# First cross attention of a two-layer perceiver: its first two batches prepared in the latents' program, the last context rows' chain earlier, the bias tile by tile

## The reference, cut to what matters

```python
xn = layernorm(x, ln_x_g, ln_x_b)          # context, 257 rows a batch
ln = layernorm(latents, ln_l_g, ln_l_b)    # latents, 32 rows a batch
q = ln @ Wq
kv = concat([xn @ Wkv, ln @ Wkv], axis=1)  # keys and values of both
qn = rmsnorm(q, qn_g) * scale
kn = rmsnorm(k, kn_g)
attn = softmax(qn kn^T)                    # mask is all ones
out = attn @ v
return out @ Wout + bout
```

## Time and profile before

| | |
|---|---|
| median of 3 runs | 2802.11 us (2801.28 to 2806.9) |
| profiled execution | 2826.43 us, span 2824.7 us |
| mean granted TensorE clock | 0.943 |
| PE busy | 2516.9 us, 89% |
| DVE, ACT, POOL busy | 60%, 45%, 52% |
| latents' program | 0 to 219.8 us |
| first cross attention's preparation | 219.8 to 277.7 us |

### The profile page before, as it was taken

How to read it: one execution, slowest core, us unless ns; L and a number is a source line. 1 busy time by engine, 2 the same in 40 slices (tenths; PEclk the granted TensorE clock), 3 DMA queues, 4 the chain that set the end, 5 groups by cost and what they waited for, 6 DMA issues and landing times. The chain is left out here.

```text
span 2824.7 us, 67316 instructions
## 1 busy us (share of the span) xinstructions
PE 2516.9 (89%) x24481; PEld 1963.2 (70%) x24481; DVE 1708.8 (60%) x3971; ACT 1280.7 (45%) x2967; POOL 1459.7 (52%) x1623
## 2 busy tenths in 40 slices
PE   5884999999999999999687989489999999998986
PEld 2443878787878787877465568378888888885654
DVE  5663767575757675866366653456556656554662
ACT  3551646464646464656243323144454444543431
POOL 4774757575757474767364135455456543322220
PEclk9996999999999999999798899799999999999995
DMA  4332111121111111111000629542234323210000
GB/s 147 126 116 66 44 34 44 30 46 28 46 28 46 29 46 33 42 37 28 26 4 4 216 78 294 173 134 88 81 96 99 80 69 72 75 33 15 3 4 30
DMA packets 221891, 190.06 MB, mean 67 GB/s; under 512 B 88513, under 2 KB 208979, under 8 KB 221587
## 3 DMA queue, kind: packets, MB, share of 16 engines
q1 hardware_dynamic: 205442, 150.88, 18.0%
q0 software_dynamic: 10656, 31.05, 4.6%
q10 hardware_dynamic: 5488, 3.94, 0.5%
HBM read 151.49 MB, written 34.31 MB: 66 GB/s over the span
## 5 line engine op out<-in xcount | busy, mean ns | idle before, releaser
L840 POOL TENSOR_TENSOR rk<-ss,neg_half 128x32 f32<-128x32 f32 x64 | 347.6, 5432 | 211.8 <-DVE ss L746 211.8
L940 ACT ACTIVATE score<-score,ntop 128x289 f32<-128x289 f32 x256 | 135.4, 530 | 255.4 <-DVE ntop L757 252.6
L1024 PE MATMUL banks<-x_hi,wk_hi 128*128 128x256 f32 x1024 | 219.5, 297 | 32.1 <-DVE kT L740 31.4
L1544 PE MATMUL banks<-rowsT,qk 128*128 128x257 f32 x1024 | 243.1, 380 | 0.8 <-ACT qk L1471 0.8
L1024 PE MATMUL banks<-x_hi,wk_lo 128*128 128x256 f32 x1024 | 211.4, 289 | 0.0
L1024 PE MATMUL banks<-x_lo,wk_hi 128*128 128x256 f32 x1024 | 210.6, 288 | 0.0
L1544 PEld LDWEIGHTS banks<-rowsT,qk 128*128 128x128 f32 x1024 | 189.4, 190 | 27.8 <-ACT qk L1471 1.5
L740 DVE COPY kT<-banks 128x512 f32<-128x512 f32 x256 | 176.1, 688 | 52.5 <-PE banks L1024 50.9
L918 ACT ACTIVATE ksq<-kT 128x512 f32<-128x512 f32 x256 | 161.2, 630 | 85.6 <-DVE kT L740 83.7
L1024 PEld LDWEIGHTS banks<-x_hi,wk_hi 128*128 128x128 f32 x1024 | 163.9, 197 | 35.6 <-DVE kT L740 25.5
L1365 POOL DMA_INDIRECT parts<-scratch_expert,address x128 | 131.7, 1029 | 93.5 <-DVE residual L1263 45.9
(11 more groups left out here) (375 smaller groups left out, 6645.7 us busy)
## 6 DMA issues: line engine op xcount, KB each, us to landing
rowsT<-in_ctxT SPq DMA_DIRECT2D x64, 257.0 KB
raw<-in_ctx SPq DMA_DIRECT2D x64, 256.0 KB
wgu<-in_expert_gu SPq DMA_DIRECT2D x64, 256.0 KB
rows<-in_ctx SPq DMA_DIRECT2D x64, 256.0 KB
scratch_qT<-qT SPq DMA_DIRECT2D x16, 512.0 KB, 2.6
scratch_kT<-kT SPq DMA_DIRECT2D x16, 512.0 KB, 3.2
q<-scratch_qT SPq DMA_DIRECT2D x64, 128.0 KB
kT<-scratch_kT SPq DMA_DIRECT2D x64, 128.0 KB
```

The source lines that it names most:

```text
L840: nc.gpsimd.tensor_tensor(m.rk[:], m.ss[:], kit.neg_half[:, 0:KF * H], ALU.pow).then_inc(s.rk, 1)
L940: nc.scalar.activation(m.score[:, c, :], m.score[:, c, :], ACT.Exp, bias=m.ntop[:, c:c + 1], accum_out=m.mass[:, c:c + 1]).then_inc(s.p, 1)
L1024: mm = nc.tensor.matmul(key_bank[i % 2][:, a * ROWS:(a + 1) * ROWS], w[:, f, pr * P:(pr + 1) * P], x[:, k, f, :], start=(at == 0), stop=(a ...
L1544: mm = nc.tensor.matmul(score[h][:, c - h * HALF, 0:CTX], m.qk[:, f, j, c * BT:(c + 1) * BT, :].rearrange("p h q -> p (h q)"), m.rowsT[:, ...
```

## The change

It moves the cross program's preparation into the latents' program, moves the last rows' chain from steps 14 and 15 to steps 0 to 3, and cuts the bias add in tiles.

- The buffers, semaphores and PSUM banks of the preparation go into a class `KeyedFront` made outside both programs, and its pieces into functions (`keyed_vector`, `keyed_pool`, `keyed_scalar`, `keyed_tensor`) that both programs call. Their bodies are unchanged. Only `keys` takes the banks as an argument; keys of batch 0 use PSUM banks 2 and 3 of the latents' program.
- In the latents' program steps 0 to 3 are written out, steps 4 to 13 stay a loop, and what is left of 14 and 15 is interleaved with the preparation.
- `high` (a temporary for the split of `wk`) now lies in the front's `kT` buffer, and takes the last rows' squares and keys too.
- The add over all of `X` goes; DVE adds `bo` to one tile at the end of each step, four at the end.
- The first batches' loads come from SP ahead of `sel` (raw 0 and 1), from ACT (raw 2, 3, 4) and from SP behind the stores (queries, keys, tails of batches 0 and 1).
- The self attention's weights are loaded by SP after group 0. `prob` is cleared and parts of batch 0 are made at the start of the cross program.

```diff
 SP, latents' program
+                front.raw(sp, 0, 0)
+                front.raw(sp, 1, 1)
                 sp.dma_start(m.sel[:], d.sel).then_inc(s.sel_in, 16)
...
+                sp.wait_ge(fs.set, 5)
+                for n in range(2):
+                    front.batch(sp, n, n)
+                for n in range(2):
+                    front.stack(sp, n, n)
 DVE, latents' program
-                def step(n, k, u, ahead):
+                def step(n, k, u):
+                    normed(n + 2, k)
                     keys(n, k)
+                    query_sums(n + 1, 1 - k)
                     queries_T(n, k, u + 1)
+                    key_sums(n + 1, 1 - k)
+                    queries(n + 1, 1 - k)
+                    if not isinstance(n, int) or n >= 2:
+                        biased(n + (-2))
...
                 normed(0, 0)
                 normed(1, 1)
+                f.norm_stats(0, 0, 1)
+                f.norm_stats(1, 1, 1)
                 query_sums(0, 0)
...
+                dve.wait_ge(cross.loaded, cross.count)
+                step(0, 0, 0)
+                f.norm_rows(0, 0, 0)
+                step(1, 1, 0)
+                f.norm_rows(1, 1, 1)
+                step(2, 0, 1)
                 dve.wait_ge(s.kl_sq, 1)
+                nc.vector.tensor_reduce(m.ssl[:], m.high[0:B, 0, :].rearrange("p (h e) -> p h e", h=H), AX.X, ALU.add).then_inc(s.kl_ss, 1)
+                step(3, 1, 1)
                 dve.wait_ge(s.rkl, 1)
                 dve.wait_ge(s.kl_copied, 1)
+                scaled(m.high[0:B, 1, :], m.rkl[:], s.klh)
                 dve.wait_ge(s.klT_ps, 1)
                 nc.vector.tensor_copy(kit.last_kT[:].rearrange("p a b -> p (a b)"), kit.psum(1)).then_inc(s.klT, 1)
+                with dve.Fori(2, NT // 2 - 1) as u:
+                    for k in range(2):
+                        step(u * 2 + k, k, u)
+
+                n, u = NT - 2, NT // 2 - 1
+                keys(n, 0)
+                query_sums(n + 1, 1)
+                queries_T(n, 0, u + 1)
+                f.norm_stats(2, 0, 2)
+                f.rows_low(0, 0)
+                key_sums(n + 1, 1)
+                queries(n + 1, 1)
+                for t in range(n - 2, n + 2):
+                    added = biased(t)
+                added.then_inc(fs.x_add, 1)
+                f.keys(0, 0, 0, early_banks)
+                f.keys(0, 0, 1, early_banks)
+                keys(n + 1, 1)
+                f.norm_stats(3, 1, 2)
+                queries_T(n + 1, 1, u + 1)
+                f.keys(0, 0, 2, early_banks)
+                f.keys(0, 0, 3, early_banks)
+                f.norm_rows(2, 0, 2)
+                f.rows_low(1, 1)
+                f.norm_rows(3, 1, 3)
+                f.key_sums(0)
+                f.keys(1, 1, 0)
+                f.norm_stats(4, 0, 3)
+                for i in range(1, front.KEYS):
+                    f.keys(1, 1, i)
+                f.rows_low(2, 0)
+                f.key_sums(1)
 POOL, latents' program (five memsets of the front first)
                 low(0, 0, 1)
                 low(1, 1, 1)
+                f.rstd(0, 0)
+                f.rstd(1, 1)
                 inverse_norms(0, 0)
+                step(0, 0, 0)
+                step(1, 1, 0)
...
+                step(2, 0, 1)
+                hold(pool, s.kl_ss, 1, s.passed)
+                inv_root(nc, pool, kit.neg_half[0:B, 0:H], m.rkl[:], m.ssl[:], 1.0 / DH, 1e-16, ALU.max, s.rkl_scaled, 1, s.rkl)
+                step(3, 1, 1)
...
+                with pool.Fori(2, NT // 2 - 1) as u:
+                    for k in range(2):
+                        step(u * 2 + k, k, u)
+                inverse_norms(NT - 1, 1)
+                hold(pool, s.klT, 1, s.passed)
+                f.last_key(0, 0)
+                f.last_key(1, 1)
+                f.rstd(2, 0)
+                f.rstd(3, 1)
+                f.key_norms(0)
+                f.key_norms(1)
 ACT, latents' program
+                step(0, 0, 0)
+                last_rows()
+                step(1, 1, 0)
+                last_squares()
+                step(2, 0, 1)
+                step(3, 1, 1)
...
+                act.wait_ge(fs.cent, 2 * KF)
+                front.raw(act, 2, 0)
+                front.raw(act, 3, 1)
                 query_squares(NT - 1, 1)
                 key_squares(NT - 1, 1)
+                f.rows_high(0, 0)
                 queries_T(NT - 2, 0, NT // 2)
                 keys_T(NT - 2, 0, NT // 2)
+                f.key_squares(0, 0, 0)
+                f.key_squares(0, 0, 1)
                 queries_T(NT - 1, 1, NT // 2)
                 keys_T(NT - 1, 1, NT // 2)
+                f.key_squares(0, 0, 2)
+                f.key_squares(0, 0, 3)
+                f.rows_high(1, 1)
+                f.key_sums(0)
+                act.wait_ge(fs.cent, 3 * KF)
+                front.raw(act, 4, 0)
...
 PE, latents' program
+                step(0, 0)
+                pe.wait_ge(s.lastn, 1)
+                pe.wait_ge(s.lnT, 3)
+                for part in range(FC):
+                    mm = nc.tensor.transpose(kit.psum(0)[:, part * B:(part + 1) * B], m.lastn[:, part * P:(part + 1) * P], kit.ident[0:B, 0:B])
+                mm.then_inc(s.lastT_ps, 1)
+                pe.wait_ge(s.lastT, 1)
+                step(1, 1)
+                pe.wait_ge(s.q_copied, 3)
+                product(m.lastT, B, 4, m.wk, s.kl_ps)
+                pe.wait_ge(s.kl_copied, 1)
+                step(2, 0)
+                step(3, 1)
+                pe.wait_ge(s.klh, 1)
+                pe.wait_ge(s.kT, 4 * 2)
+                for a in range(NP_):
+                    mm = nc.tensor.transpose(kit.psum(1)[:, a * B:(a + 1) * B], m.high[0:B, 1, a * P:(a + 1) * P], kit.ident[0:B, 0:B])
+                mm.then_inc(s.klT_ps, 1)
+                pe.wait_ge(s.klT, 1)
...
+                f.rows_T(0, 0)
+                queries_T(NT - 2, 0)
+                keys_T(NT - 2, 0)
+                pe.wait_ge(s.k_copied, NT)
+                f.keys(0, 0, 0, early_banks)
+                f.keys(0, 0, 1, early_banks)
+                queries_T(NT - 1, 1)
+                f.keys(0, 0, 2, early_banks)
+                keys_T(NT - 1, 1)
+                f.keys(0, 0, 3, early_banks)
+                f.rows_T(1, 1)
+                f.key_sums(0)
+
+                pe.wait_ge(s.qT_high, NT)
                 pe.wait_ge(s.kT, NT * 2)
+                f.keys(1, 1, 0)
+                f.sums_T(0)
+                for i in range(1, front.KEYS):
+                    f.keys(1, 1, i)
+                f.rows_T(2, 2)
+                f.key_sums(1)
+                f.sums_T(1)
 cross program
 SP
                 group(0, lambda j: True)
+                sp.wait_ge(plain.zeroed, 1)
+                plain.load(sp)
 DVE
                 dve.wait_ge(s.set, 6)
-                nc.vector.tensor_tensor(X[:], X[:], wm.bo[:].unsqueeze(1).to_broadcast([P, NT, D]), ALU.add).then_inc(s.x_add, 1)
                 groups(dve, group)
```

More of the change, by code:

```diff
@@ L184, in latent_queries @@
+def latent_queries(kit, cross, front, ahead):
     nc, d = kit.nc, kit.dram
@@ L535, in keys_T, with step @@
                     columns(m.key[:, k, HP * P:INNER], 6, P, s.kT_ps)
[L537 to L543 removed]
+                def step(n, k):
+                    queries(n + 1, 1 - k)
+                    rows_T(n + 2, k)
+                    keys(n + 1, 1 - k)
                     queries_T(n, k)
@@ L562, in _ @@
-                pe.wait_ge(s.q_copied, NT)
-                product(m.lastT, B, 4, m.wk, s.kl_ps)
-                step(NT - 1, 1, 0)
-                pe.wait_ge(s.klh, 1)
-                pe.wait_ge(s.kT, NT * 2)
-                for a in range(NP_):
-                    mm = nc.tensor.transpose(kit.psum(1)[:, a * B:(a + 1) * B], m.key[0:B, 0, a * P:(a + 1) * P], kit.ident[0:B, 0:B])
-                mm.then_inc(s.klT_ps, 1)
+                step(0, 0)
+                pe.wait_ge(s.lastn, 1)
+                pe.wait_ge(s.lnT, 3)
@@ new lines, in _ @@
+                pe.wait_ge(s.kT, 4 * 2)
[3 more added lines that the diff above has]
+                pe.wait_ge(s.klT, 1)
+                with pe.Fori(2, NT // 2 - 1) as u:
+                    for k in range(2):
+                        step(u * 2 + k, k)
+                queries(NT - 1, 1)
+                keys(NT - 1, 1)
@@ L702, in _ @@
             def _(dve):
-                dve.wait_ge(weights.loaded, weights.count)
-                def norm_stats(n, k, loads):
-                    if isinstance(n, int):
-                        past(dve, s.aggr, n * KF)
-                    dve.wait_ge(raw_in[k], loads * 16)
-                    for c in range(KF):
-                        nc.vector.bn_stats(m.stats[:, c, :], m.raw[:, k, c, :]).then_inc(s.stats, 1)
-                    hold(dve, s.stats, (n + 1) * KF, s.passed_dve)
-                    for c in range(KF):
-                        nc.vector.bn_aggr(m.mv[:, k, c, :], m.stats[:, c, :]).then_inc(s.aggr, 1)
@@ L1054, in spread @@
```

(12 more changed lines are left out.)

575 lines of the change are left out of this document (274 added, 301 removed).

## The result

| | before | after |
|---|---|---|
| median | 2802.36 us (2801.28 to 2806.9, 4 runs) | 2755.01 us (2746.97 to 2766.89, 4 runs) |
| profiled execution | 2826.43 us, span 2824.7 | 2746.97 us, span 2745.2 |
| mean granted TensorE clock | 0.943 | 0.962 |
| PE's first mask product of the loop | 277.74 | 250.12 |
| from there to the last group's (groups 0 to 6) | 967.4 us | 951.8 us |

The ratio is 0.9833, 95% interval 0.9813 to 0.9854: 47 us less. That is faster, as forecast, but outside the range of 2761 to 2788.

A forecast was written before the change was run, and what follows sets the result against it. PE bounds the whole span, but idles before the cross attention's loop, where a DVE and POOL chain sets the pace. Loop start 236.2 + 13.3 = 249.5 against 277.74, scaled to a gain of 28.0, gave 2774 us; range 2761 to 2788.

The forecast's parts named there:

- Start: Beginning of the latents' program: added fills, raw loads, statistics and small roots fit in existing waits and cost nothing.
- Last rows' chain: Latents' steps 0 to 3: the moved chain makes engines wait in order, 13.3 us late by the root of keys 5.
- Rival 2: Last rows' chain mostly hidden at the start: 3 us late, gain 38, time 2764 us; chance 0.14.
- Bias by tile: Latents' sixteen steps: each tile's bias add takes 0.4 us on DVE and costs nothing in the loop.
- rival 4: Latents' steps: each bias add holds up POOL's power by 0.4 us, 4.8 in all, time 2779 us; chance 0.07.
- Tail: From the root of keys 15 (208.8) to the cross attention's loop start at 236.2, before adding the last rows' lateness.
- Rival 3: Tail draws out by 5 us and the last rows' chain costs 18: gain 18, time 2784 us; chance 0.13.
- Moved to after: Fill of `prob`, parts 0 and load issues, moved into or behind the cross program's start, cost nothing; without cover 6 us.
- Sum: Loop start at 236.2 + 13.3 = 249.5 against 277.74, 28.2 us earlier; time 2774 us.
- first part: Opening section on what bounds the kernel: PE overall, but idle before the cross attention's loop; an earlier loop start moves everything behind.
- an equal length from there to the end: Expected sign in the profile after: from PE's first mask product to the end takes as long as before.
- groups after the first: Cross attention's loop: the prediction counted itself wrong if these groups came out longer.

The follow-up runs named there:

- second profile: The changed kernel measured and profiled once more, nothing altered, as the mark for another set: 2762.01 us against 2806.31 of before, ratio 0.9831.
- before with sixteen: The kernel before with sixteen semaphore increments added on DVE in the latents' program, ahead of its loop: 2807.13 us against 2821.71, ratio 0.9953.
- after with seventy-six: The changed kernel with seventy-six semaphore increments added on DVE ahead of the latents' loop: 2781.04 us, ratio to before 0.9912.
- 8, 2 and 128 more: Three runs: the kernel before with that many semaphore increments added on DVE in the latents' program: 2810.26 us (8), 2804.95 us (2), 2807.81 us (128).
- 90 more: The changed kernel with ninety semaphore increments added on DVE ahead of the latents' loop: 2779.59 us, ratio to before 0.9852.
- before with thirty-two: The kernel before with thirty-two semaphore increments added on DVE ahead of the latents' loop: 2806.59 us.

## Why the prediction was right and wrong

- **Start**: as said, nothing. The first root of keys ended within 0.6 us of before.
- **Last rows' chain**: roots of keys 2, 3, 4 and 5 forecast to end at 69.35 (64.8 + 1.31 + 2.96 is 69.07; the row that I wrote out lacks 0.3), 83.9, 96.6 and 113.9; measured 70.2, 85.1, 97.8 and 114.9. Forecast 13.3 us late against before, measured 14.3 at keys 5 and 13.9 at keys 15. PE's queries 2, 3 and 5 were forecast at 55.2, 69.85 and 97.5 and came at 54.43, 71.07 and 98.40. Rival 2 (3 us late) is out; leaving the chain out gave 15.0 us.
- **Bias by tile**: 0.42 us each for the forecast 0.4, and nothing in the steps. The step became even shorter, 10.78 for 10.82, since POOL's power took 2.92 where it was 2.96, here over the steps of the loop:

```profile
L122 POOL TENSOR_TENSOR rq<-rq,neg_half 128x16 f32<-128x16 f32 x10 | 29.2, 2922 | 0.8
L122 POOL TENSOR_TENSOR rk<-rk,neg_half 128x16 f32<-128x16 f32 x10 | 29.2, 2922 | 0.8
```

  A bias add on DVE that ran from 187.13 to 187.55 overlapped the power that POOL began at 187.43, which took its 2.92 us all the same. So rival 4, and with it a lock for the whole instruction as the Trainium skill has it (SBUF — State Buffer, "SBUF: two separate sides"), did not show. With the bias alone, where all sixteen adds stand in the steps, the root of keys 15 ended at 206.96, not 5 us later but 1.8 us earlier than before's 208.8, and the loop started 6.3 us earlier, of which 4.4 are the add. Of the 1.8 us some 0.5 are the shorter steps; 1.3 were there by the end of the root of keys 1 (56.09 for 57.39), and no run here tells why.
- **Tail**: forecast 27.4 us from the root of keys 15 to the loop (208.8 to 236.2), measured 27.4 (222.68 to 250.12). Rival 3 is out.
- **Moved to after**: nothing, as said; the first batch of group 0 took 16.17 us, and 16.13 in the kernel before.
- **Sum**: loop start 249.5 forecast, 250.12 and 249.6 measured. The errors (+1.0 at keys 5, -0.4 by the shorter step) leave 0.6.
- **The step that failed** is the first part's "Whatever shortens the way to the loop's first instruction moves everything behind it", and with it "an equal length from there to the end" and "groups after the first". I took the loop as fixed. It became 15.7 us shorter (13.7 in the second profile), because the change put 52 more instructions ahead of it in DVE's stream. Padding alone, in either direction, moves about the same amount: 17.6 us less for before with sixteen, 14.7 more for after with seventy-six (against the changed kernel's second profile). This part of the gain was luck of placement and no merit of the moved work: 2755 instead of 2774 is mostly this.

The account: 27.6 to 28.1 us at the start and 13.7 to 15.7 in groups 0 to 6 make 42 to 43, against medians that differ by 47 and 44 (41 to 52 and 40 to 55 by the intervals). The rest is inside the intervals. Behind the groups the profiled executions differ by more than that: from group 7 to the router's program 310.3 us before, 302.4 after and 310.0 in the changed kernel's second profile; the experts' program took 124.1 in before's profile, 111.4 in after's, 111 in all profiles of the first set (8, 2 and 128 more, last rows left out) and of the third (76 more and all runs below it), and 123 to 126 in all of the second (16, 32 and 90 more, loop written out), before's code and after's alike.

What stays open is the 0.07 us by which the batches behind each group's second became longer. A pair of key products comes every 0.240 us instead of 0.237, written out or not; no run here tells why.

## What to carry to other kernels

An edit ahead of a loop moves the loop's own code in each engine's instruction list, and that alone was worth 14 to 18 us of 2800 here, about a third of the whole gain. Where a trace shows "issue" waits just behind a jump back, pad the stream and measure again (here eight made it worse and sixteen better), or write the loop out, before crediting or blaming an edit; and when two versions are compared, compare the landmarks before the loop, the first batch behind each jump, and the other batches apart. Count the place in the compiled list, not in the source.

## What the runs showed of the hardware

- After a jump back over a loop of 484 instructions DVE stood still for 3.2 to 3.5 us, and for 1.4 to 2.5 us more where one of the borders, 128 instructions apart, lay within the loop's first ten or so (2.1 to 2.9 more where both waits fell together). Written out, the same code had neither. Borders further inside cost little: 0.15 to 0.25 us where one lay 8 to 10 instructions behind a batch's first score operation (before's third batch, the fifth with sixteen, the seventh with thirty-two), 0.36 in after's second batch (15 behind), and nothing in the third batch of before with two (6 behind).
- The page of the profile counts the transfers. Its part 3 has, for before with sixteen increments and for after:

```profile
q14 instruction: 91, 0.75, 0.1%
```

```profile
q14 instruction: 130, 1.06, 0.1%
```

  Each packet is 8.2 KB (1.06 MB by 130), which is 64 bytes for each of 128 instructions. Before had 98 of them and 91 with sixteen increments, seven fewer, one for each pass through the loop: by the borders at 214, 342, 470 and 598 its 484 instructions lie in five pieces in before and in four with sixteen more, and the trace has six and five packets a pass, one more than the pieces in each case. The count does not tell of the stall, though: the changed kernel has 130 with the second stall (seventy-six more) and without it. It has eleven packets a pass, more than DVE's five pieces, so this queue seems to serve another engine too; that was not traced.
- The Trainium skill (Advanced Engine Details and Errata, "ISA Cache") gives an engine other than TensorE an instruction cache of 32 KB in two lines of 16 KB, or 256 instructions. The 64 bytes an instruction agree. The size of the piece does not: with borders every 256, seventy-six increments would have brought nothing back and 128 would not have repeated before. On DVE the measured piece is half the page's. With borders at 214, 470 and 726, two lines of 256 would have held the whole loop of before with sixteen, yet five packets moved in each of its passes. The other queue's packets are 16.4 KB (3.41 MB by 208 in after).
- What a stall cost on top of itself depended on the clock granted behind it, and the length of PE's wait did not decide that by itself. Without a second stall PE waited up to 2.7 us for DVE's copy, and the 12 us around the end of the wait mostly had 1.00 (first batches of 17.5 to 17.9 us) or 0.86 (19.0 to 19.5): 0.86 with a wait of 1.75 (before with thirty-two, group 1), 1.00 with one of 2.68 (last rows left out, group 6). With a second stall (before, and after with seventy-six) it waited 3.2 to 4.1 us and had 0.72 or 0.86, and once 1.00 (3.28 us, after with seventy-six, group 5; batch 19.3).
